# Self-attention of a perceiver layer: 1024 value columns and a separate output product, in place of 2048 value columns that hold the output product

## The reference

```
x = x + xattn(layernorm(x), ctx_1024, lens)   # 16 heads of 64, 1601 context rows a batch
x = x + attn(layernorm(x))                    # self-attention, this is what changes
x = x + ffn(layernorm(x))                     # 384 hidden, with quantised values

def attn(y):                                  # y: (32, 64, 128)
    qkv = y @ w_qkv                           # (128, 3 * 1024)
    q, k, v = split into 3, 16 heads of 64
    s = where(mask, q k^T / 8, -inf)          # with 64 tokens the mask is the causal one
    o = softmax(s) v                          # (32, 64, 1024), heads side by side
    return o @ w_out                          # (1024, 128)
```

## Time and profile before

| | |
|---|---|
| median of 3 runs | 2385.29 us (2382.2 to 2387.34) |
| the profiled execution | 2382.76 us, of which the span in the trace is 2380.9 us |
| mean granted TensorE clock | 0.998 of full speed |
| TensorE busy | 2316.4 us (97%) |
| VectorE busy | 2104.1 us (88%) |
| ScalarE busy | 1384.2 us (58%) |
| GpSimd busy | 1494.4 us (63%) |
| self-attention | from 2050.28 us (the first instruction of its block) to 2291.18 us (the end of its last) |

### The profile page before, as it was taken

The page is one execution under the profiler, slowest core; times in us unless marked ns, Lnnn a source line. Parts: engine busy times, 40 slices in busy tenths (PEclk is TensorE's granted clock), DMA queues, the critical chain, the costliest instruction groups (busy, mean ns, idle before and its releaser), DMA issues. The chain is left out here.

```text
span 2380.9 us, 57755 instructions
## 1 busy us (share of the span) xinstructions
PE 2316.4 (97%) x16519; PEld 1970.4 (83%) x16519; DVE 2104.1 (88%) x3367; ACT 1384.2 (58%) x2594; POOL 1494.4 (63%) x1085
## 2 busy tenths in 40 slices
PE   7989999999999999999999999999999999999988
PEld 4757888888888888888888888888888888878756
DVE  7799999999999999999999999999999998568777
ACT  6845555555555555555555555555555554455646
POOL 4557777777777777777777777777777773001100
PEclk9999999999999999999999999999999999999999
DMA  3422222222222222222222222222222223531000
GB/s 117 191 77 50 55 54 54 53 54 54 54 54 55 54 54 54 55 54 54 54 54 54 53 54 54 54 54 54 54 54 54 54 48 107 166 107 38 2 2 18
DMA packets 442653, 145.07 MB, mean 61 GB/s; under 512 B 365360, under 2 KB 425680, under 8 KB 442448
## 3 DMA queue, kind: packets, MB, share of 16 engines
q1 hardware_dynamic: 442432, 143.50, 24.3%
q10 hardware_dynamic: 144, 0.52, 0.1%
HBM read 109.17 MB, written 34.73 MB: 60 GB/s over the span
## 5 line engine op out<-in xcount | busy, mean ns | idle before, releaser
L471 POOL TENSOR_TENSOR probs<-arena,best_all 128x1024 f32 (+2 forms) x397 | 943.5, 2377 | 428.5 <-DVE best L848 407.1
L1114 PEld LDWEIGHTS u_ps<-rows,probs 128*128 128x128 f32 x6656 | 802.8, 191 | 49.0 <-ACT probs L678 8.8
L1114 PE MATMUL u_ps<-rows,probs 128*128 (+1 forms) x6656 | 809.4, 275 | 7.9 <-ACT probs L678 4.9
L678 ACT ACTIVATE probs<-probs 128x1024 f32<-128x1024 f32 (+1 forms) x416 | 440.8, 1061 | 473.4 <-POOL probs L471 460.1
L833 DVE SCALAR_TENSOR_TENSOR arena<-s_ps,mask,rrms 128x512 f32 (+2 forms) x832 | 611.0, 735 | 96.5 <-PE s_ps L979 94.1
L636 ACT ACTIVATE squares<-k_ps 128x512 f32<-128x512 f32 (+1 forms) x832 | 474.2, 594 | 143.7 <-PE k_ps L979 120.3
L808 DVE TENSOR_REDUCE ssq<-squares 128x16 f32<-128x1024 f32 (+2 forms) x416 | 491.1, 1180 | 37.0 <-ACT squares L636 34.7
L848 DVE TENSOR_TENSOR best<-best,arena 128x1024 f32<-128x1024 f32 (+1 forms) x352 | 449.1, 1276 | 0.1
L977 PE MATMUL k_ps<-w_hi,cT_hi 128*128 128x512 f32 (+1 forms) x832 | 363.7, 437 | 0.5 <-ACT squares L636 0.4
L977 PE MATMUL s_ps<-q_hi,cT_hi 128*128 (+2 forms) x832 | 330.1, 397 | 8.7 <-DVE arena L833 7.5
L979 PE MATMUL s_ps<-q_hi,cT_lo 128*128 (+2 forms) x832 | 328.9, 395 | 0.0
(11 more groups left out here) (258 smaller groups left out, 2230.2 us busy)
## 6 DMA issues: line engine op xcount, KB each, us to landing
stage<-in_ctx SPq DMA_DIRECT2D x1536, 16.0 KB, 1.7
rows<-in_ctx SPq DMA_DIRECT2D x32, 768.0 KB
queries<-probs SPq DMA_DIRECT2D x16, 1024.0 KB, 4.0
q_plain<-queries SPq DMA_DIRECT2D x32, 512.0 KB, 3.3
best_all<-best_rows SPq DMA_DIRECT2D x31, 512.0 KB, 3.8
u_transposed<-uT_sb SPq DMA_DIRECT2D x124, 128.0 KB, 2.6
a_uT<-u_transposed SPq DMA_DIRECT2D x10, 1024.0 KB, 4.9
arena<-u_transposed SPq DMA_DIRECT2D x6, 1024.0 KB, 4.9
```

Source lines behind the costliest of these rows:

```text
L471: pool.tensor_tensor(probs[0:r, slot_of(c, PRING), :], scores_at(b, c), best_all[0:r, bass.ds((b % 2) * HL, HL)], ALU.subtract).then_inc(s ...
L678: act.activation(tile, tile, ACT.Exp).then_inc(probs_ready.sem, 1)
L1114: last = pe.matmul(u_ps[g // 3][:, at:at + UW], probs[0:r, s, g * P:(g + 1) * P], rows, start=(c == 0 and g % 3 == 0), stop=(c == NC - 1), ...
```

## The change

`wvo2` goes, with its transposes, its product, its saves and its split into two parts of 2048 columns. `Wv2` itself is split (`wv_hi`, `wv_lo`, 1024 columns each), so that `project_v` fills two banks instead of four, and these are now `tp`. `mix` exchanges its operands: values are the stationary one, probabilities the moving one, and the result `o` stands transposed, with one bank for each batch of the tile. ScalarE saves it as `oT` (`save_oT`, two instructions), and a new `project_o` multiplies it by `w_out` (8 products of 128 x 128 on 128 columns, added up in one bank); VectorE adds one bank instead of two. The order in a step changes to `turn_p`, `sum_heads`, `turn_y`, `mix`, `project_v`, first half of `project_qk`, `project_o`, second half of `project_qk`, `score`. `four` becomes `work[0]`, `work[1]`, `tp[0]`, `tp[1]`. `w_out` lies in another piece of the arena and is loaded once chunk 8 of batch 30 has been shifted. ScalarE saves `oT` behind `yT_hi` up to step 5, and ahead of the exponential from step 6 on.

```
-    "wout": at(5, 1), "wvo": at(6, 2), "wvo2": at(8, 2), ... "v2": [at(0, 2), at(2, 2)],
+    "wout": at(8, 1), "wvo": at(6, 2), ... "v": [at(0, 1), at(1, 1)],
...
+                    sp.wait_ge(shifted.sem, shifted.ended((B - 2) * NC + 8))
                     sp.dma_start(w_now["wout"].rearrange("p (g o) -> p g o", o=D), ...
...
-            save_wvo2()
...
-                if ending(p) and c < 4:
+                if ending(p) and c < 2:
                     save_turned_weights(c)
...
-                for banks, w in ((k_ps, w_now["wv"]), (s_ps, w_now["wqkv"][:, 2 * HL:3 * HL])):
-                    for g in range(PAIRS):
-                        last = pe.transpose(banks[g // 4][:, ...
+                for h in range(2):
+                    for g in range(4 * h, 4 * h + 4):
+                        last = pe.transpose(k_ps[h][:, (g % 4) * P:(g % 4 + 1) * P], w_now["wv"][:, g * P:(g + 1) * P], ident[:, :])
...
             each_step(pe, query, step)
-            multiply_weights("wv2T", "wout", wvo_saved)
...
-        four = (*tp, *work)
+        four = (*work, *tp)
...
+            def save_oT(t):
+                for b in range(2):
+                    act.wait_ge(mixed, 2 * t + b + 1)
+                    act.activation(oT[:, :].rearrange("p (g b q) -> p b g q", b=2, q=L)[:, b],
+                                   ov[b][:, :].rearrange("p (g q) -> p g q", q=L), ACT.Copy).then_inc(oT_saved, 1)
...   # ScalarE, step(i)
+                if i + SUM_AHEAD >= TILES:
+                    save_oT(i)
                 t = i + 1
                 if 0 <= t < TILES:
                     act.wait_ge(shifted, t + 1)
...
+                if 0 <= i < TILES - SUM_AHEAD:
+                    save_oT(i)
+                t = i + V_AHEAD
+                if 0 <= t < TILES:
+                    for k in range(2):
+                        act.wait_ge(v_ps, 2 * t + k + 1)
+                        act.activation(w["v"][t % 2][:, half(k)], tp[k][:, :], ACT.Copy).then_inc(v_saved, 1)
...
-                    dve.wait_ge(mixed, 2 * t + 2)
+                    dve.wait_ge(o_projected, t + 1)
                     link(dve.tensor_tensor(x2[:, cols(t)], ov[0][:, 0:D], x1[:, cols(t)], ALU.add))
-                    link(dve.tensor_tensor(x2[:, cols(t)], ov[1][:, 0:D], x2[:, cols(t)], ALU.add))
...   # mix
-                            last = pe.matmul(ov[r][b * L:(b + 1) * L, 0:D], w["pT"][rows, at:at + L],
-                                             w["v2"][t % 2][rows, odd * HL + g * D:odd * HL + (g + 1) * D],
-                                             start=(g == 0), stop=(g == PAIRS - 1))
+                            last = pe.matmul(ov[b][odd * HD:(odd + 1) * HD, g * L:(g + 1) * L],
+                                             w["v"][t % 2][rows, odd * HALF + g * HD:odd * HALF + (g + 1) * HD],
+                                             w["pT"][rows, at:at + L], start=True, stop=True)
...
+            def project_o(t):
+                pe.wait_ge(oT_saved, 2 * t + 2)
+                for g in range(PAIRS):
+                    last = pe.matmul(ov[0][:, 0:D], oT[:, g * P:(g + 1) * P], w["wout"][:, g * D:(g + 1) * D],
+                                     start=(g == 0), stop=(g == PAIRS - 1))
+                last.then_inc(o_projected, 1)
...   # project_qk(j, r, i, parts)
+                for k in parts:
+                    pe.wait_ge(qk_saved, max(0, parts_upto(i - 1) - 3 + k))
+                    if k == 0:
+                        pe.wait_ge(added, upto(i, SUM_AHEAD))
+                    elif k == 1:
+                        pe.wait_ge(yT_lo_ready, 2 * upto(i, TURN_Y_AHEAD))
+                    else:
                         pe.wait_ge(pT_saved, 2 * upto(i, 0))
+                        pe.wait_ge(v_saved, max(0, 2 * upto(i, V_AHEAD) - 3 + k))
...   # project_v
-                for k in range(4):
+                for k in range(2):
...   # TensorE, step(i)
+                if 0 <= i + TURN_Y_AHEAD < TILES:
+                    turn_y(i + TURN_Y_AHEAD, i)
                 if i >= 0:
                     mix(i)
-                if 0 <= i + TURN_Y_AHEAD < TILES:
-                    turn_y(i + TURN_Y_AHEAD, i)
+                if 0 <= i + V_AHEAD < TILES:
+                    project_v(i + V_AHEAD, i)
                 j, r = qk_part(i)
                 if 0 <= j < QK_PARTS:
-                    project_qk(j, r, i)
-                if 0 <= i + V_AHEAD < TILES:
-                    project_v(i + V_AHEAD, i)
+                    project_qk(j, r, i, (0, 1))
+                if i >= 0:
+                    project_o(i)
+                if 0 <= j < QK_PARTS:
+                    project_qk(j, r, i, (2, 3))
                 if 0 <= i + S_AHEAD < TILES:
                     score(i + S_AHEAD)
```

More of the change, by code:

```diff
@@ L1121, in turn_weights, with multiply_weights @@
                 pe.wait_ge(last_columns, 2)
-                for banks, w in ((k_ps, w_now["wv"]), (s_ps, w_now["wqkv"][:, 2 * HL:3 * HL])):
-                    for g in range(PAIRS):
-                        last = pe.transpose(banks[g // 4][:, (g % 4) * P:(g % 4 + 1) * P], w[:, g * P:(g + 1) * P], ident[:, :])
+                for h in range(2):
+                    for g in range(4 * h, 4 * h + 4):
+                        last = pe.transpose(k_ps[h][:, (g % 4) * P:(g % 4 + 1) * P], w_now["wv"][:, g * P:(g + 1) * P], ident[:, :])
                     last.then_inc(post_turned, 1)
-            def multiply_weights(turned, w, saved):
+            def multiply_weights():
                 for k, banks in enumerate((k_ps, s_ps)):
@@ L1130, in multiply_weights @@
                         for odd in range(2):
-                            if j == 0:
-                                pe.wait_ge(saved, 2 * k + odd + 1)
                             rows = slice(odd * HD, (odd + 1) * HD)
                             g = slice((4 * k + j) * D, (4 * k + j + 1) * D)
-                            last = pe.matmul(banks[odd][:, j * D:(j + 1) * D], w_now[turned][rows, g], w_now[w][rows, g],
+                            last = pe.matmul(banks[odd][:, j * D:(j + 1) * D], w_now["wvT"][rows, g], w_now["wo"][rows, g],
                                              start=True, stop=True)
@@ L1546, in mix @@
             def mix(t):
[L1547 removed]
+                pe.wait_ge(v_saved, 2 * t + 2)
                 pe.wait_ge(x2_ready, t)
@@ L1587, in project_v @@
                 pe.wait_ge(yT_lo_ready, 2 * t + 2)
-                pe.wait_ge(wvo2_ready, 4)
-                for k in range(4):
-                    pe.wait_ge(qk_saved, max(0, parts_upto(i) - 3 + k) if parts_upto(i) > parts_upto(i - 1) else parts_upto(i))
+                pe.wait_ge(wv_ready, 2)
+                for k in range(2):
                     if k == 0:
-                        pe.wait_ge(v_saved, 4 * t)
+                        pe.wait_ge(qk_saved, parts_upto(i - 1))
+                        pe.wait_ge(v_saved, 2 * t)
                         pe.wait_ge(pT_saved, 2 * upto(i, 0))
-                        pe.wait_ge(added, upto(i, SUM_AHEAD))
-                        pe.wait_ge(yT_lo_ready, 2 * upto(i, TURN_Y_AHEAD))
-                    tokens = window(t, k // 2)
-                    pe.matmul(four[k][:, :], yT_hi[:, tokens], wvo2_hi[:, half(k)], start=True, stop=False)
-                    pe.matmul(four[k][:, :], yT_lo[:, tokens], wvo2_hi[:, half(k)], start=False, stop=False)
-                    pe.matmul(four[k][:, :], yT_hi[:, tokens], wvo2_lo[:, half(k)], start=False, stop=True).then_inc(v_ps, 1)
+                    tokens = window(t, k)
+                    pe.matmul(tp[k][:, :], yT_hi[:, tokens], wv_hi[:, half(k)], start=True, stop=False)
+                    pe.matmul(tp[k][:, :], yT_lo[:, tokens], wv_hi[:, half(k)], start=False, stop=False)
+                    pe.matmul(tp[k][:, :], yT_hi[:, tokens], wv_lo[:, half(k)], start=False, stop=True).then_inc(v_ps, 1)
             def score(t):
```

75 lines of the change are left out of this document (29 added, 46 removed).

## The result

The changed kernel took 2391.15 us, the median of 13 runs (2387.03 to 2395.41), beside 2385.36 for 13 runs of the kernel before: ratio 1.0025, 95% interval 1.0017 to 1.0034. It is slower by 5.8 us, just more than the 0.2% that can be told from no change. The forecast was 2391.0. Its profiled execution took 2389.42 with a span of 2387.6, where the sum of the prediction said 2388.5. (I count from the profiled executions: 2389.42 - 2382.76 = +6.7, predicted +5.75.)

The account below looks back on a forecast made before the run. Bound: TensorE's work and an almost equally long chain through VectorE's split; softmax in steps 11 to 15. Terms -2.1 + 1.4 - 1.8 + 3.0 + 1.3 - 0.8 + 4.75 = +5.75 us: profiled 2388.5, median 2391.0, range 2382.5 to 2399.5.

Parts of the forecast that it names:

- TensorE's work: Each self-attention step: two value banks fewer (-1.4), shorter mix (-0.82), added project_o (+1.79); -0.4 us a step without waits.
- The rival that the mix doesn't get shorter: Row halves take turns writing one bank, so mix stays at 1.9 us; +14.1 in all, 2399.4; chance 0.10.
- The wait at the split: Steps 0 to 5: TensorE's second query/key bank waits 0.65 us for VectorE's yT_lo, about 1 in steps 1 to 3; +3.0.
- the late quantisation: Steps 1 to 3: VectorE's quantisation starts behind project_o, making VectorE late by another 0.3 us.
- The score wait: Steps -2, 2, 6 and 10: score waits for ScalarE's save of the last key bank, 0.8 us each.
- Warm-up: Steps -5 to -3: three banks follow the split instead of one, +0.45 us each, +1.4; steps -2 and -1 together -1.8.
- End of cross-attention: Second multiply_weights and its saves go, so the block ends 2.1 us earlier; eight removed weight transposes gain nothing.
- The load of `w_out`: Before the cross-attention weight transposes: later load costs nothing; rival: it lands late, transposes wait 3.5 us, 2394.5, chance 0.05.
- Step 6: Split comes when it did, but 6.0 us instead of 4.73 lie from that bank to step 7; +1.3 us.
- The tail: Steps 11 to 15: oT saves delay the exponential, and later project_o delays turn_p(15) and VectorE's addition; +4.75 us.
- the removed work returning in full: Whole kernel: TensorE's work is the path and ready work covers the waits; -6.4 us, 2378.9; chance 0.13.
- The one of about the same: Half of the tail's 4.75 us or the score waits are hidden; +2 to +3.5 us, 2387 to 2389; chance 0.26.

Follow-up runs that it names:

- experiment 1: Changed kernel with project_o moved ahead of all four banks of queries and keys: 2385.34 us, ratio 1.0005 to the kernel before.
- experiment 6: Changed kernel with the bank order of the kernel before and project_v moved behind project_qk and project_o, before score: 2379.43 us, ratio 0.9981 to the kernel before.
- experiment 7: Changed kernel in the order of the kernel before: mix before turn_y, four project_qk banks together, then project_o, project_v, score: 2387.14 us, ratio 1.0010 to the kernel before.
- Experiment 4: Changed kernel with project_o behind the fourth bank of queries and keys in steps 2, 6 and 10 only: 2389.64 us, ratio 1.0019 to the kernel before.
- experiment 9: Changed kernel with eight removed transposes of self-attention's value weights put back, their results unread: 2389.83 us, ratio 1.0023 to the kernel before.
- late_exponential_first: Changed kernel with ScalarE's exponential ahead of the oT saves, score ahead of project_o and a later addition in steps 12 to 15: 2391.43 us, ratio 1.0031.
- experiment 3: Changed kernel with sixteen identity transposes between the first two banks of queries and keys in step 6: 2390.76 us, ratio 1.0026 to the kernel before.

## Why the prediction was right, and where its sum was not

- **TensorE's work** (-0.4 a step): right. `mix` 1.09 as predicted from the score's shape, `project_o` 1.70 for 1.79. The rival that the mix doesn't get shorter is out: `mix` takes the same 1.09 as `score`, 17 ns an instruction. The Trainium skill ("TensorEngine Tiling (Array Packing)", Gotcha 1: PSUM Pressure) says that different row tiles can't access the same bank at once; this trace shows no time lost to it, as the 64 instructions took the same 1.09 us.
- **The wait at the split**: right, and experiments 1, 6 and 7 show it on the path. Its size in steps 4 and 5 was 0.57 and 0.55 for 0.65. In steps 1 to 3 I had about 1; it was 0.70, 0.69 and 0.56, so that the late quantisation is a term of at most 0.15, not 0.3. Hence +2.5 for +3.0.
- **The score wait** (0.8): 0.69 in each of steps -2, 2, 6 and 10. Experiment 4 gets back 0.78 in step 2 and 0.34 in step 10; in step 6 the clock is mixed in.
- **Warm-up**: the mechanism right, +0.6 a step for +0.45.
- **End of cross-attention**: -2.1, as predicted. That the removed transposes return nothing is shown by experiment 9. The reason I gave was a late exponential; in the trace after, TensorE first waits for ScalarE's division, and it is the same cover by ScalarE:

```profile
2016.13 1.04 PE L1115 MATMUL k_ps<-ident,arena 128*128 128x128 f32 x8
2017.66 3.53 PE L1105 MATMUL u_ps<-rows,probs 128*128 128x129 f32 x26 [0.49 <-ACT u_sb L653]
```

- **The load of `w_out`**: never near the path. It was issued at 2004.80 and landed after 5.3 us, half of the 11.0 in the earlier trace rows, which it had spent in company; the rival of a late load is out.

```profile
arena<-in_L_attn_w_out SPq DMA_DIRECT2D x1, 512.0 KB, 5.3
```

- **Step 6**: the step that was mis-sized, +1.3 for +2.9. Where the clock held (late_exponential_first, transposes_back) the step takes 12.92, which is +1.2 on the earlier trace rows and what I had; the other 1.6 is `project_o` and the banks around it at the lower clock. I named a lower clock as what would make the forecast wrong, but looked for it in the tail, where pauses of up to 1.6 us leave it at 1.00, and not at the step where a wait of 1.19 was about to become one of 2.15.
- **The first sum**: the other term missing, +1.7 in this profile, for the same reason: without the second `multiply_weights` TensorE pauses 0.58, 0.75 and 1.65 us with little work between. That the change brought this fall is argued, not shown: the kernel before has 3.71 in only two profiles.
- **The tail**, steps 12 to 15 (+4.75): mechanism right, size +3.6. The exponential of step 12 started 3.59 us in for 3.9:

```profile
2266.95 1.09 ACT L1362 ACTIVATE a_oT<-a_ov 128x512 f32<-128x512 f32 x2 [0.84 <-PE a_ov L1562]
2267.92 1.06 ACT L1378 ACTIVATE a_p_odd<-a_p_odd 128x1024 f32<-128x1024 f32 x1
```

so the step grew by 0.55 for 0.85, step 13 shrank by 0.15 where I had +0.2, and step 14 grew by 1.3 for 1.6. From `turn_p(15)` to VectorE's addition there were 5.8 us (2289.38 to 2295.16) for 6.0.

The terms I left out, two falls of the clock (+3.3), met a main loop, a tail and steps 0 to 5 that were smaller than I had them (-2.4 with the small terms), and so the sum came out 0.9 off. A second error hid this one: I had the median 2.5 above the profiled execution, as in the kernel before, and it lies 1.7 above. That the median was met to 0.15 us is luck; the sign was not. Of the rivals, the removed work returning in full fails at the split. The one of about the same was nearer than its text: not through a hidden score wait, which was measured, but because without the two falls the profiled difference would be +3.4, at its upper end.

## What to carry to other kernels

When a change shortens work that stands in front of a wait, ask whose result that wait is for and where the wait will be met next; the gain goes there first. Here some 11 us lay in the order of the pieces of one engine's step and their banks (1.0026 against 0.9981 in the same runs), with the same instructions. Before moving a piece behind a wait, list what is queued behind it on its own engine and on the engine that consumes it: the same late product gained 0.8 us in one step and cost 1.5 in the next, and in step 14 it cost 4.2, of which 2.7 were the clock that fell during the wait. Where a change lengthens a wait to some 2 us, look for the clock behind it.

## What the runs showed of the hardware

TensorE's granted clock fell to its lower level behind idle stretches of some 2 us, and not in every execution: the same code with a wait of 2.18 us was followed by `project_o` at 3.05 in one profile and at 1.95 in two. In the self-attention of all fourteen profiles there are nine waits of 2.05 to 2.58 us, and the clock fell behind six of them. It also fell behind pauses of 0.58, 0.75 and 1.65 us close together, in five of nine profiles, while pauses of up to 1.6 us in the tail of the changed kernel left it at 1.00. The Trainium skill ("TensorE: Matmul & The Clock Gate", Part 1: The HAM clock gate) says that one and the same kernel runs a different number of products at the lower level at its start from run to run; I did not read that start, but these profiles show the like in the middle of a kernel. Filling the stretch with transposes of the identity went with 1.95 and 3.71 in every profile that had them (4 of 4), although they do nothing for the result. A remedy of that kind has to be judged over many executions: its price in one profile (1.6 us) was not found in the median of eight runs of experiment 3.
